# Values two units back moved directly behind the scores, and reciprocals and selected heads moved ahead of the evacuations, in a decoder attention loop

## What is computed

```
h = mha(x, x, saw, sab, mask);   x = layer_norm(h + x, ...)   # self-attention
h = mha(x, enc, caw, cab, None); x = layer_norm(h + x, ...)   # cross-attention over 257 keys
h = relu(x @ W1 + B1) @ W2 + B2; x = layer_norm(h + x, ...)   # MLP, 256 -> 1024 -> 256
```

## Time and profile before

| what | value |
|---|---|
| median of three runs | 5195.07 us (5189.7 to 5195.42) |
| the profiled execution, its time | 5196.5 us |
| its span | 5194.3 us |
| decoder layers in it | about 970 to 3206 us |
| PE busy | 4231.0 us, 81% of the span |
| PEld busy | 3145.5 us, 61% |
| DVE busy | 2779.0 us, 53% |
| ACT busy | 1882.7 us, 36% |
| mean granted TensorE clock | 0.896 of full |

### The profile page before, as it was taken

One profiled execution on the slowest core, in us unless ns is written; L12 is line 12 of the kernel. 1 busy time (PEld: TensorE's weight loads), 2 busy tenths in 40 slices (PEclk: granted clock), 3 DMA queues, 4 the chain that ended last, 5 costly groups with the idle time before them and its releaser, 6 DMA issues. The chain is left out here.

```text
span 5194.3 us, 96901 instructions
## 1 busy us (share of the span) xinstructions
PE 4231.0 (81%) x39298; PEld 3145.5 (61%) x39298; DVE 2779.0 (53%) x5804; ACT 1882.7 (36%) x5127; POOL 308.7 (6%) x562
## 2 busy tenths in 40 slices
PE   6996695799999899999999997539588777877763
PEld 4664585577777677677677775338445576555533
DVE  2335411566666666666666674751267545244447
ACT  1222131344444344444444443102166444244421
POOL 0000101000000000000000000010111000000000
PEclk9998798899999999999999998859799788888876
DMA  2000165201101101101101100018544200000000
GB/s 99 26 26 18 51 221 191 68 26 44 50 18 44 51 26 36 51 26 36 51 30 40 50 18 16 1 51 294 183 153 148 90 0 22 17 17 24 9 1 8
DMA packets 112157, 302.45 MB, mean 58 GB/s; under 512 B 28856, under 2 KB 74616, under 8 KB 87168
## 3 DMA queue, kind: packets, MB, share of 16 engines
q1 hardware_dynamic: 108672, 288.28, 16.3%
q0 software_dynamic: 3072, 8.39, 0.5%
HBM read 281.68 MB, written 14.94 MB: 57 GB/s over the span
## 5 line engine op out<-in xcount | busy, mean ns | idle before, releaser
L2264 ACT ACTIVATE layers_probs<-banks,layers_negmax 128x257 f32<-128x257 f32 x768 | 358.2, 472 | 1156.4 <-DVE layers_negmax L2148 1156.4
L2000 PE MATMUL banks<-weights_a,ctx_tiles 128*128 128x256 f32 x1536 | 389.1, 386 | 92.2 <-ACT layers_sa_nT L2237 92.2
L1994 PE MATMUL banks<-ctx_tiles,weights_a 128*128 128x257 f32 x1536 | 406.6, 388 | 0.0
L2000 PEld LDWEIGHTS banks<-weights_a,ctx_tiles 128*128 128x128 f32 x1536 | 284.1, 192 | 143.2 <-ACT layers_sa_nT L2237 108.8
L2054 PE MATMUL banks<-layers_KT,layers_qblk 32*64 32x257 f32 x3072 | 267.1, 418 | 47.2 <-issue 25.5
L1994 PEld LDWEIGHTS banks<-ctx_tiles,weights_a 128*128 128x128 f32 x1536 | 274.3, 194 | 46.4 <-issue 18.9
L2128 DVE TENSOR_TENSOR layers_V<-banks,rows_a 128x256 f32<-128x256 f32 x384 | 160.3, 418 | 265.5 <-PE banks L2000 265.4
L2148 DVE TENSOR_REDUCE layers_negmax<-banks 128x2 f32<-128x514 f32 x384 | 262.3, 683 | 63.5 <-PE banks L2054 63.3
L2062 PEld LDWEIGHTS banks<-const,layers_probs 128*128 128x128 f32 x1536 | 169.5, 146 | 158.5 <-issue 158.4
L2062 PE MATMUL banks<-const,layers_probs 128*128 128x128 f32 x1536 | 265.1, 298 | 0.0
L2269 ACT COPY layers_pT<-banks 128x512 f32<-128x512 f32 x384 | 223.8, 583 | 3.3 <-PE banks L2062 3.3
(11 more groups left out here) (709 smaller groups left out, 8623.2 us busy)
## 6 DMA issues: line engine op xcount, KB each, us to landing
ctx_tiles<-in_ctx SPq DMA_DIRECT2D x66, 1028.0 KB, 4.9
weights_a<-in_L_w SPq DMA_DIRECT2D x44, 1024.0 KB, 5.3
l2x_B<-positions SPq DMA_DIRECT2D x32, 1280.0 KB, 5.9
weights_b<-in_L_w SPq DMA_DIRECT2D x32, 1024.0 KB, 6.4
weights_c<-in_L_w SPq DMA_DIRECT2D x16, 1024.0 KB, 7.2
weights_b<-in_L_xattn_w SPq DMA_DIRECT2D x12, 1024.0 KB, 7.4
ctx_tiles<-in_ctx_keys SPq DMA_DIRECT2D x32, 256.0 KB, 2.9
weights_c<-in_sa_w SPq DMA_DIRECT2D x24, 256.0 KB, 2.8
```

What stands on the lines that cost most here:

```text
L1994: last = mm(o[:, 0:LK], ca_wk[:, c, m * P:(m + 1) * P], E.ctx[:, tile % 2, c, j * LK:(j + 1) * LK], start=c == 0, stop=c == DC - 1)
L2000: last = mm(o[:, 0:D], E.ctx[:, tile % 2, c, first:first + P], ca_wv[:, c], start=c == 0, stop=c == DC - 1)
L2264: a(probs[:, cc, j, t], ps[:, t, 0:LK], ACT.Exp, bias=negmax[:, k % 2, t:t + 1], accum_out=totals[:, cc, t, j:j + 1]).then_inc(s["exp_done ...
```

## The change

Two reorderings, in PE's and in DVE's sequence of an iteration. No instruction is added or removed, no shape, buffer, wait or DMA is edited.

```diff
                     for it in range(N * U):
                         if ca_unit(it):
                             scores(it, *ca_unit(it))
+                        if ca_unit(it - 2):
+                            values(*ca_unit(it - 2))
                         if ca_unit(it - 1):
                             transposes(*ca_unit(it - 1))
                         for a in jobs_in(it):
                             job(*a)
-                        if ca_unit(it - 2):
-                            values(*ca_unit(it - 2))
...
                         if ca_unit(it):
                             maxima(*ca_unit(it))
-                        for a in jobs_in(it):
-                            take(*a)
                         if ca_unit(it - 1):
                             if (it - 1) % GB == GB - 1:
                                 reciprocals(*ca_unit(it - 1))
                         if ca_unit(it - 2) and (it - 2) % GB == GB - 1:
                             own_heads(*ca_unit(it - 2))
+                        for a in jobs_in(it):
+                            take(*a)
                         if it == first_ca * U + 2:
```

## The result

The kernel after takes 5223.59 us (median of five runs, 5212.87 to 5227.58). The kernel before, run again beside it, takes 5189.7 us (5182.41 to 5195.42). The ratio is 1.0061, with a 95% interval of 1.0045 to 1.0076: slower by 0.6%; the forecast was 5223 us and 0.5%. The two profiled executions, 5196.5 us before and 5223.59 us after, differ by 27.1 us; the forecast had worked out 28.1 us against the same 5196.5. The medians differ by 33.9 us, because the runs of before beside it came out 5.4 us lower than the three the forecast started from, whose profiled execution was itself 1.4 us above their median. The runs of the kernel after spread over 15 us, so a forecast that meets their median within 1 us owes that to luck; what can be held against the forecast are its terms.

The account below looks back on a forecast made before the run. PE was taken to bound the kernel, busy 2091 of 2236 us, except in two stretches set by DVE and ACT. 5196.5 + 19.1 (moved values) + 9 (clock) = 5224.6, less 1.4 for the median: 5223 us, range 5201 to 5243.

Parts of the forecast that it names:

- The circle of stretches: PE's step around the DVE/ACT-set stretches: one values block more in PE-set work, 0.36 us, 53 times, 19.1 us.
- V1's wait: V1's matmuls in unit u0 wait for ACT's copy of S0: stays 2.26 us, about 41 times.
- Y to u4: From Y's matmuls to unit u4's scores, set by DVE and ACT: length unchanged, PE's stall grows from 0.13 to 0.49 us.
- New neighbours at 0: PE's hand-overs between tile shapes: scores to values 0.59 us, values to transposes 0.36; net 0, bounds 32 us down or up.
- rival of a cheaper hand-over: PE's scores-to-values hand-over 0.11 us cheaper, 32 us less, 5191 us; chance 0.06.
- hidden anyway: Rival: Y's chain shortens or moved values meet unseen slack; about 5200 us if half is lost, 5195 if all; chance 0.07.
- New waits at 0: PE's waits for the values' copy, selected heads and reciprocals cost nothing; tightest in unit u4, fitting by 0.18 us.
- DVE at 0: DVE's evacuations queue behind heads or reciprocals in units u0, u1, u4, u5, but delay no critical chain: 0 us.
- The clock: TensorE's clock falls behind waits for S0, 1.5 us each: six more, 9 us, bounds -30 to +30 us.
- a fall behind every wait: Rival: TensorE's clock falls after each of the 41 S0 waits, +30 us, 5244 us; chance 0.06.

Follow-up runs that it names:

- Undoing u2 alone: Kernel after, with the values behind the jobs again in unit u2 only, as before: 5190.53 us, ratio to before 1.0.
- without the two DVE chains: Second part of each layer norm moved behind the next unit's maxima on DVE: 5040.77 us on the kernel before, 5038.75 us on the kernel after.
- PE's half alone: Kernel before with only PE's reordering, DVE's order as before: 5377.16 us, ratio 1.0373.
- a longer step without new idle time: Kernel before, with 12 of the values' matmuls done a second time in unit u6: 5223.88 us, ratio 1.0069.
- DVE's half: Kernel before with only DVE's reordering, PE's order as before: 5493.27 us, ratio 1.0586.

## Why the prediction was right

*The circle of stretches* (19.1 us) held: V1's wait unchanged at 2.26 us, Y to u4 unchanged at 6.78 us with one block less in it, the short step longer by 0.37 (forecast 0.36), all of it idle time of PE. The five stretches from the last V1 of one layer to the first of the next hold three such blocks each, 1.08 us by the forecast. The first and the third of them, before and after:

```profile
1291.31:1389.43 98.12, 91.08 (x940) 68.96 (x940) 63.36 (x141) 40.46 (x131) 5.30 (x12) 0.95 0.07 20
2045.28:2147.16 101.88, 91.16 (x940) 69.11 (x940) 63.33 (x141) 40.45 (x131) 5.30 (x12) 0.93 0.07 21
```

```profile
1297.42:1396.62 99.20, 91.10 (x941) 68.77 (x941) 63.56 (x141) 40.73 (x131) 5.32 (x12) 0.95 0.07 21
2061.55:2162.20 100.65, 88.61 (x940) 67.21 (x940) 63.56 (x141) 40.62 (x131) 5.31 (x12) 0.95 0.07 22
```

PE's idle time (length less PE busy) grew by 1.06 us in the first, 1.32 in the third, and 5.8 us in all five, where the forecast has 5.4. Undoing u2 alone took the loss away, and the values early in u0 alone made a gain, and without the two DVE chains the order no longer matters.

*New neighbours at 0* held: 0.59 and 0.36 us, and the two orders within 2 us of each other without the chains. The rival of a cheaper hand-over falls with that; the rival "hidden anyway" too.

*New waits at 0, DVE at 0*: no wait on the heads, the shares or a bank has come, and the copy fits. PE's half alone shows what this cover is worth: 3.6 us a step.

*The clock* (9 us, six falls more) was the weakest term. In the 34 countable steps eight falls more have come, 12 us at 1.5; in the five stretches across the layers' ends the same instructions kept PE busy 4.3 us less than before (451.7 against 456.0 us), most of it in the third, where the mean granted clock rose from 0.93 to 0.95. So the clock cost some 8 us. The number was right, but nothing in the forecast had worked it out: it was a choice between two bounds, and a fall behind every wait did not come either (10 of the 34 steps are short). Of the two reasons given for the choice, more idle time was not the cause: a longer step without new idle time brings eight more as well. For the long steps that come in pairs no run was made. Added up: 34 x 0.36 + 8 x 1.5 + 1.6 (by which the five stretches grew, 502.6 to 504.2) = 26 us of the 27.1.

## What to carry to other kernels

Where an engine waits at a fixed point for a chain on other engines, work placed between the chain's start and that point is free, and the same work a little earlier or later costs its full time if this engine sets the pace there. So look for such stretches before reordering, and count which blocks enter and leave each one; an order that is right in one unit of the loop is wrong in another. Better still, look at what stands in the chain and needn't: here the second part of a layer norm stood ahead of the next unit's maxima, and moving it behind these gained 2.9%, more than five times what the best placing of the values that was tried did (0.5%, with the reciprocals moved too).

## What the runs showed of the hardware

A repeated idle time of about 2.3 us in a stretch of 45 us was followed by the lower TensorE clock (granted clock 0.50, about 1.5 us lost) in some repetitions and not in others, and how many differed with the length of the repetition: 16 of 34 at 45.37 us (twice), 24 of 34 at 45.73 and at 45.83 us, and with the wait at 1.89 us 16 of 34 at 45.18 and 10 of 34 at 45.00 us, each counted in one execution. That a longer repetition always brings more falls is not shown. In the kernels with no such wait there was none inside a layer: each of the 39 steps between Ys of one layer has 42.72 or 42.73 us at a granted clock of 1.00. A change that lengthened the step by 0.4 us cost, in the 34 steps, about as much again through the clock (12 us for the 12 us of the steps).

The lower clock lengthened PE's busy time and not its waits. In the kernel with DVE's half, whose three waits make 7 us of idle time in each step, a step took 50.43 us at full clock and 54.63 at a mean granted clock of 0.91, with the same idle time; the extra 4.2 us are all PE busy.
